# Graph attention: where the exponential is written, and how many PSUM banks the scores have

## The reference

```python
h = jnp.maximum(_layernorm(x, axis=-1), 0.0)
q = h @ Wq.T + bq
k = h @ Wk.T + bk
v = h @ Wv.T + bv
a = q @ k.T * (1.0 / sqrt(256)) + adj + adj
out = x + jax.nn.softmax(a, axis=-1) @ v
```

## Time and profile before

| | |
|---|---|
| median of three runs | 862.66 us |
| the profiled execution | 862.07 us |
| its span, first to last instruction | 860.0 us |
| PE busy (matmul) | 819.8 us, 95% |
| DVE busy | 592.9 us, 69% |
| POOL busy | 394.8 us, 46% |
| ACT busy | 343.5 us, 40% |
| DMA, mean | 95 GB/s |
| mean granted clock of TensorE | 0.988 |

### The profile page before, as it was taken

One profiled execution on the slowest core, in us unless ns is written; L12 is line 12 of the kernel. 1 busy time (PEld: TensorE's weight loads), 2 busy tenths in 40 slices (PEclk: granted clock), 3 DMA queues, 4 the chain that ended last, 5 costly groups with the idle time before them and its releaser, 6 DMA issues.

```text
span 860.0 us, 16570 instructions
## 1 busy us (share of the span) xinstructions
PE 819.8 (95%) x6720; PEld 816.4 (95%) x6720; DVE 592.9 (69%) x986; ACT 343.5 (40%) x616; POOL 394.8 (46%) x325
## 2 busy tenths in 40 slices
PE   5766899999999999999999999999999999999998
PEld 4766799999999999999999999999999999999998
DVE  4455586767777776767777776767777677767764
ACT  2221234444434444444434344443444344443455
POOL 4255354452709082543618081634528090725445
PEclk9988899999999999999999999999999999999999
DMA  4225023232324332333323332333323243423200
GB/s 158 85 70 199 10 76 96 89 111 86 113 74 123 99 111 86 98 105 94 111 74 115 95 123 87 110 88 98 104 81 114 84 123 94 116 86 92 82 26 13
DMA packets 43708, 81.68 MB, mean 95 GB/s; under 512 B 4976, under 2 KB 5616, under 8 KB 43632
## 3 DMA queue, kind: packets, MB, share of 16 engines
q1 hardware_dynamic: 43632, 80.63, 31.1%
HBM read 76.42 MB, written 4.19 MB: 94 GB/s over the span
## 4 chain that ended last, share of the span: by engine, by line
PE 90%; POOL 4%; DVE 3%; ACT 1%; issue 1%; DMA 1%; SPq 0%; DVEq 0%; ACTq 0%
PE ps L276 44%; PE ps L362 14%; PE ps L364 14%; PE ps L363 14%; POOL x_rows L236 4%; PE ps L268 1%; DVE stats L481 1%; PE ps L342 1%; POOL rstd L231 1%; DVE ring_a L512 1%; DVE hT L491 1%; DMA x_rows<-in_x 1%; PE ps L349 0%; ACT hT L409 0%; DVE mean_var L484 0%
## 5 line engine op out<-in xcount | busy, mean ns | idle before, releaser
L276 PE MATMUL ps<-qhl,hT 128*128 128x256 f32 x3072 | 409.3, 283 | 0.1
L276 PEld LDWEIGHTS ps<-qhl,hT 128*128 128x128 f32 x3072 | 386.2, 191 | 0.3 <-DVE v L506 0.3
L252 POOL TENSOR_TENSOR ring_a<-ring_a,m_row 128x512 f32<-128x512 f32 x179 | 230.6, 1340 | 276.6 <-ACT m_row L460 276.6
L362 PE MATMUL ps<-v,p_hi 128*128 128x258 f32 x1024 | 291.2, 284 | 1.2 <-DVE x_res L551 1.2
L364 PE MATMUL ps<-v,p_lo 128*128 128x258 f32 x1024 | 288.7, 282 | 0.0
L363 PE MATMUL ps<-v,p_hi 128*128 128x256 f32 x1024 | 288.6, 282 | 0.0
L456 ACT CAST p_hi<-ps 128x512 fp32r<-128x512 f32 x256 | 150.4, 588 | 231.4 <-PE ps L364 229.4
L512 DVE TENSOR_TENSOR ring_a<-ps,ring_a 128x512 f32<-128x512 f32 x179 | 123.6, 690 | 104.3 <-PE ps L276 103.6
L362 PEld LDWEIGHTS ps<-v,p_hi 128*128 128x128 f32 x1024 | 193.9, 189 | 1.5 <-DVE x_res L551 1.4
L364 PEld LDWEIGHTS ps<-v,p_lo 128*128 128x128 f32 x1024 | 194.0, 189 | 0.0
L363 PEld LDWEIGHTS ps<-v,p_hi 128*128 128x128 f32 x1024 | 193.4, 189 | 0.0
(11 more groups left out here) (63 smaller groups left out, 357.9 us busy)
## 6 DMA issues: line engine op xcount, KB each, us to landing
ring_a<-in_adj SPq DMA_DIRECT2D x179, 256.0 KB, 2.6
ring_b<-in_adj SPq DMA_DIRECT2D x77, 256.0 KB, 2.6
x_res<-in_x SPq DMA_DIRECT2D x16, 256.0 KB, 2.9
out<-x_res SPq DMA_DIRECT2D x16, 256.0 KB, 2.0
x_rows<-in_x SPq DMA_DIRECT2D x7, 512.0 KB, 3.7
x_rows<-in_x SPq DMA_DIRECT2D x4, 128.0 KB, 3.2
w_all<-in_w SPq DMA_DIRECT2D x1, 512.0 KB, 4.4
w_all<-in_w SPq DMA_DIRECT2D x1, 256.0 KB, 4.4
```

Source lines behind the costliest of these rows:

```text
L252: nc.gpsimd.tensor_tensor(slot_tiles(w), slot_tiles(w), m, ALU.subtract).then_inc(s_sub, 1)
L276: last = nc.tensor.matmul(dst, lhs(a, ib), rhs(c, ib), start=(n == 0), stop=(n == 3 * DB - 1))
L362: nc.tensor.matmul(ps[:, O_BANK + i, 0:VW], hi, v[:, n, 0:VW], start=(n == 0), stop=False)
```

## The change

The exponential is written over its input, the logits in the slot of the ring, and p_hi and p_lo are computed from the slot. The two PSUM banks that it had go to the scores, which rotate over four banks from step 16 on (over two before that, while banks 2 and 3 hold the transposed h) and wait for the add of four steps back. The exponential no longer waits for p_lo of w - 2. SP fills a slot again when p_lo has read it, no longer when the exponential has.

```diff
--- before.py
+++ after.py
@@ -76,7 +76,7 @@
         x_res = sb("x_res", [P, QS, D])
 
         ps = ctx.enter_context(nc.psum_tensor("ps", [P, 8, BANK], f32))
-        S_BANK, E_BANK, O_BANK, A_BANK, X_BANK = 0, 2, 4, 6, 7
+        S_BANK, S_BANKS, O_BANK, A_BANK, X_BANK = 0, 4, 4, 6, 7
         HT_BANK, V_BANKS = 2, (4, 6)
 
         wqk_nat = w_all[:, 0:2 * DB * D].rearrange("p (w o i) -> p w o i", w=2, o=DB)
@@ -88,11 +88,11 @@
             n = s % RING
             return ring_a[:, n, :] if n < FIRST else ring_b[:, n - FIRST, :]
 
+        def banks(s):
+            return 2 if s < FIRST else S_BANKS
+
         def slot_tiles(s):
             return slot(s).rearrange("p (k q) -> p k q", k=KT)
-
-        def bank_tiles(n):
-            return ps[:, n, :].rearrange("p (k q) -> p k q", k=KT)
 
         s_wqk = sem("wq_wk_loaded")
         s_wv = sem("wv_biases_loaded")
@@ -157,7 +157,7 @@
         def _(sp):
             def load_adj(s):
                 if s >= RING:
-                    sp.wait_ge(s_exp, s - RING + 1)
+                    sp.wait_ge(s_plo, s - RING + 1)
                 sp.dma_start(slot(s), adj_units[s // UNITS, s % UNITS].rearrange("p k q -> p (k q)"))\
                     .then_inc(s_adj[s % RING], 16)
 
@@ -324,11 +324,11 @@
                 b, u = s // UNITS, s % UNITS
                 if u == 0:
                     pe.wait_ge(s_qlo, b + 1)
-                if s >= 2:
-                    pe.wait_ge(s_add, s - 1)
+                if s >= banks(s):
+                    pe.wait_ge(s_add, s - banks(s) + 1)
                 for k in range(KT):
                     at = (KT * u + k) * P
-                    last = split_product(ps[:, S_BANK + s % 2, k * QB:(k + 1) * QB],
+                    last = split_product(ps[:, S_BANK + s % banks(s), k * QB:(k + 1) * QB],
                                          lambda a, ib: hT[:, a, ib, at:at + P],
                                          lambda c, ib: qhl[:, b % 2, c, ib, :])
                 last.then_inc(s_score, 1)
@@ -445,15 +445,13 @@
 
             def exponential(w):
                 act.wait_ge(s_sub, w + 1)
-                if w >= 2:
-                    act.wait_ge(s_plo, w - 1)
-                nc.scalar.activation(ps[:, E_BANK + w % 2, :], slot(w), ACT.Exp, scale=2.0).then_inc(s_exp, 1)
+                nc.scalar.activation(slot(w), slot(w), ACT.Exp, scale=2.0).then_inc(s_exp, 1)
 
             def write_p_hi(w):
                 act.wait_ge(s_exp, w + 1)
                 if w >= PB:
                     act.wait_ge(s_pv, w - PB + 1)
-                nc.scalar.copy(p_hi[:, w % PB], bank_tiles(E_BANK + w % 2)).then_inc(s_phi, 1)
+                nc.scalar.copy(p_hi[:, w % PB], slot_tiles(w)).then_inc(s_phi, 1)
 
             def keep_max(b):
                 act.wait_ge(s_bcast, b + 1)
@@ -509,7 +507,7 @@
             def add_adj(s):
                 dve.wait_ge(s_score, s + 1)
                 dve.wait_ge(s_adj[s % RING], 16 * (s // RING + 1))
-                nc.vector.tensor_tensor(slot(s), ps[:, S_BANK + s % 2, :], slot(s), ALU.add).then_inc(s_add, 1)
+                nc.vector.tensor_tensor(slot(s), ps[:, S_BANK + s % banks(s), :], slot(s), ALU.add).then_inc(s_add, 1)
 
             def running_max(s):
                 b, u = s // UNITS, s % UNITS
@@ -539,7 +537,7 @@
 
             def write_p_lo(w):
                 dve.wait_ge(s_phi, w + 1)
-                nc.vector.tensor_tensor(p_lo[:, w % PB], bank_tiles(E_BANK + w % 2), p_hi[:, w % PB].bitcast(f32),
+                nc.vector.tensor_tensor(p_lo[:, w % PB], slot_tiles(w), p_hi[:, w % PB].bitcast(f32),
                                         ALU.subtract).then_inc(s_plo, 1)
 
             def finish(b):
```

## The result

The changed kernel takes 870.12 us (median of 4 runs, 868.82 to 870.33) against 862.75 us for the kernel before in the same sitting: a ratio of 1.0082, 95% interval 1.0065 to 1.0100, so 7.4 us slower. The profiled execution took 870.17 us, with a span of 868.3 us.

A forecast was written before the change was run, and what follows sets the result against it. The prediction took PE (TensorE) as the bound, so only its delays cost time. Finish 3.5, drain 3.4 and first burst 1.2 gave 8.1 us, with a few tenths +8.3: 871.0 us against the 862.66 us median; range 866 to 877 us.

The forecast's parts named there:

- The banks: Score groups on PE: four score banks give nothing, taken as 0, at most 4.8 us of hidden gaps.
- The rival that they pay: Score groups on PE: hidden gaps go and outweigh the port's cost, 858 us at best; chance 0.04.
- ACT: In-place exponential and cast to p_hi: 0.06 us a step at most, covered by ACT's idle time, so nothing.
- Queues: SP's loads: later slot reloads arrive in time; a late x_res pauses POOL some 2 us; cost 0.
- The wait at the port: p_lo on VectorE, both inputs in SBUF, waits for POOL at the shared port in each of 16 bursts.
- W: The wait of one p_lo for POOL to release the port, between 0 and 1.16 us.
- Rival (a): At the port: each engine waits for the other's whole instruction, 1.99 us per pair, about 880 us; chance 0.10.
- Finish: Head of a block: late finish idles PE 0.25 us, bounds 0 and 0.8; fourteen blocks, 3.5 us.
- Drain: Only weightings left on PE: p_lo paced by POOL, 1.69 against 1.43 us, 13 times, 3.4 us; bounds 0 and 5.
- First burst: First weightings: p_lo's wait goes straight to PE, 0.9 and 0.3 us, together 1.2 us.
- Rival (b): At the port: not slower, p_lo slips between POOL's operations, lag within 3.5 us of slack, 863 us; chance 0.11.
- Rival (d): In each block: p_lo's 3.5 us slack runs out, 0.5 us or more each, 880 us and above; chance 0.02.

The follow-up runs named there:

- e1_two_banks: The changed kernel with the scores rotating over two banks only, the exponential still in place: 869.77 us, ratio 1.0094.
- e2_short_pool: The changed kernel with POOL's subtraction of the maximum cut from 512 to 8 columns, the rest left out: 861.18 us, ratio 0.9990.
- e3_late_reload: The kernel before, with SP refilling a slot after p_lo instead of after the exponential: 861.82 us, ratio 1.0000.
- e8_two_outputs: The changed kernel with two score banks, the two freed banks given to the output, so PE waits for the finish of two blocks back: 866.87 us, ratio 1.0057.
- e6_drain_psum: The changed kernel with the last block's exponential put back into PSUM banks 2 and 3: 866.89 us, ratio 1.0057.
- e10_paced_pool: The changed kernel with POOL's subtraction of unit w, outside the last block, waiting for p_lo of w - 2: 865.26 us, ratio 1.0046.
- e7_both: The changed kernel with the edits of e5_finish_first and e6_drain_psum joined: 867.18 us, ratio 1.0064.
- e5_finish_first: The changed kernel with VectorE's finish moved ahead of the add of the same step: 869.33 us, ratio 1.0089.

## Why the prediction was right

The forecast was 871.0 us, the measured time 870.12 us. The mechanism and its three places came as told, each term a little larger than forecast. By its steps:

- **The banks: 0.** Shown by e1_two_banks. The rival that they pay falls with it.
- **ACT: 0.** The two instructions grew by 26 and 33 ns, together the 0.06 us that was the upper bound; e2_short_pool shows it hidden.
- **Queues: 0.** SP's waits name p_lo, as foreseen, and e3_late_reload prices the later release at nothing. POOL waits for x_res once a block, 2.4 us in the mean (33.9 us, 14 times), about where the 2 us were put.
- **The wait at the port.** The hand-worked schedule gave W = 1.1 and 1.0 us for the first two p_lo; the rows give 1.77 and 1.71 us, less 0.68. Rival (a), the lock of the full instruction, would have had POOL's operation and p_lo 1.99 us apart in the drain; they are 1.70 us apart, so it falls.
- **Finish: 0.25 a block forecast, 0.29 measured**, 14 times, so 3.5 and 4.1 us; e8_two_outputs shows that it is this wait. The 0.1 us for the start of a semaphore wait had no row behind it; the weighting at 411.18 starts 0.16 us late, and its next matmul costs another 0.1 us.
- **Drain: 3.4 forecast, 3.57 measured**, shown by e6_drain_psum.
- **First burst: 1.2 forecast (0.9 and 0.3), 1.40 measured.** The first weighting starts 5.24 us behind the first copy and 4.15 us before, so 1.1 us later; the next three steps, at VectorE's pace, add 0.3 us. Then q's projection gives PE other work and p_lo catches up. e8_two_outputs keeps this term, and e10_paced_pool takes it away.

Without the prelude the profiles differ by 5.45 + 3.57 = 9.0 us; the sum said 8.3, of which 0.2 us stood for nothing in particular, and the medians say 7.4. So that the total came within 1 us is in part luck. The range of 866 to 877 us does not follow from the bounds that were given for the terms, which reach from about 863 to 880 us.

One reading of the rows was wrong. Line 524 at 0.68 us was said to have hardly anything of POOL beside it. Five of those 14 instructions start during a POOL scaling of x_rows (line 236, 128 x 256). Three of the five (46.46, 70.37, 94.29) start with it to within 0.02 us and take 0.69 to 0.72 us, while the POOL operation takes 1.73 us instead of 1.22. There it is POOL that waits. The other two (58.96, 82.89) start 0.7 us into the POOL operation, and neither takes longer. In the burst VectorE started 0.05 us behind POOL, and VectorE waited. So the rows held both outcomes, and the forecast needed the one in which VectorE comes second, which it had argued from a late VectorE being locked to POOL's ends; the changed kernel bears that out.

Rival (b), not slower, stood on p_lo slipping between POOL's operations. That nearly happens once in the stretch shown, at 411.64, with a wait of 0.17 us; it isn't the rule. Rival (d), the slack of p_lo used up in each block, was given 0.02 and did not come in this kernel: the p_lo at 413.73 ended at 415.44, with the weighting that needs it at about 417.0, so 1.6 of 3.5 us were left, and 1.5 us at the next. Only the first burst, which starts without slack, ran that way. But e7_both is that rival in its effect, at 0.25 us a block. The prediction's "3.5 us of slack holds it" was right by less than it sounded, and the expectation of e5_finish_first was wrong because it priced one wait without following VectorE's phase against POOL's past it.

## What to carry to other kernels

Before moving an operand of a VectorE instruction from PSUM to SBUF, see what GpSimd does at that time: the trace may already hold a contended instruction of the same form, and its two durations price the change. Then ask where the lateness reaches the engine that is the bottleneck; 91 us of it in the blocks cost 0.7 us in one order, and 105 us cost 5.5 us in another. If the two must share, pace the one with slack (a single wait here) before reordering the one that is late.

## What the runs showed of the hardware

- A VectorE instruction with two SBUF inputs and a GpSimd one that reads SBUF take turns, without exception in the stretches read: each late p_lo got in behind the running GpSimd operation, and the pair took 1.70 us (1.25 + 0.45), where the two alone are issued 1.25 and 0.60 us apart. In the steady part that locks VectorE, which had 0.8 us to spare per step before, to GpSimd's rhythm: its p_lo at 413.73, 416.68 and 419.64 are 2.95 us apart, two GpSimd operations and one turn. With one input in PSUM the same instruction took 0.68 us beside GpSimd. What the traces show is the waiting; that it is for a port is the reading given to it here.
- Either engine can be the one that waits. In the prelude three VectorE instructions (128 x 512, two SBUF inputs) that started with a GpSimd one (128 x 256) to within 0.02 us took 0.69 to 0.72 us and the GpSimd one 1.73 instead of 1.22 us; at the head of a burst VectorE started 0.05 us behind a GpSimd instruction of 128 x 512 and took 1.79 us. What sets which of them waits was not varied.
- On ScalarE a 128 x 512 float32 exponential took 0.604 us from SBUF to PSUM and 0.630 us in place in SBUF, a cast to SBUF 0.588 us from PSUM and 0.621 us from SBUF.
